# Seven-product down projection: another order of the products, and one activation sum on GpSimd

## The reference, cut to what matters

```python
x = x + _L0_ffn_ref(_layernorm(x, axis=-1), L0_ffn_w_gate, L0_ffn_w_up, L0_ffn_w_down)

def _L0_ffn_ref(x, w_gate, w_up, w_down):
    gate = jnp.einsum('bsd,hd->bsh', x, w_gate)
    up = jnp.einsum('bsd,hd->bsh', x, w_up)
    gated = jax.nn.silu(gate) * up
    return jnp.einsum('bsh,dh->bsd', gated, w_down)
```

## Time and profile before

| | us |
|---|---|
| runs, median of 3 | 1593.62 |
| runs, lowest to highest | 1592.47 to 1597.46 |
| profiled execution, its own time | 1592.21 |
| profiled execution, span | 1590.4 |
| TensorE busy in the span | 1528.7 (96%) |
| VectorE / ScalarE / GpSimd busy | 817.7 / 532.8 / 840.2 |

### The profile page before, as it was taken

The page is one execution under the profiler, slowest core; times in us unless marked ns, Lnnn a source line. Parts: engine busy times, 40 slices in busy tenths (PEclk is TensorE's granted clock), DMA queues, the critical chain, the costliest instruction groups (busy, mean ns, idle before and its releaser), DMA issues.

```text
span 1590.4 us, 23621 instructions
## 1 busy us (share of the span) xinstructions
PE 1528.7 (96%) x8204; PEld 1244.1 (78%) x8204; DVE 817.7 (51%) x1264; ACT 532.8 (34%) x1093; POOL 840.2 (53%) x643
## 2 busy tenths in 40 slices
PE   6999899999999999989999999999999999999998
PEld 5676688888888887777877877877877877877786
DVE  5666516235154187766256256256356346346346
ACT  3334423222132233333343343343343343343332
POOL 0000320211211302287797797797797797797794
PEclk9999999999999999999999999999999999999999
DMA  9663320110100100011111111121121221121212
GB/s 370 246 244 141 110 77 1 53 53 26 53 26 26 54 1 21 7 47 47 59 54 45 59 58 46 55 61 45 53 67 38 56 69 33 59 66 33 59 53 106
DMA packets 41798, 110.42 MB, mean 69 GB/s; under 512 B 4672, under 2 KB 4800, under 8 KB 39328
## 3 DMA queue, kind: packets, MB, share of 16 engines
q1 hardware_dynamic: 41328, 109.07, 20.3%
q10 hardware_dynamic: 432, 0.82, 0.2%
HBM read 105.68 MB, written 4.19 MB: 69 GB/s over the span
## 4 chain that ended last, share of the span: by engine, by line
PE 76%; DVE 13%; issue 5%; ACT 3%; POOL 1%; DMA 1%; DVEq 0%; SPq 0%; POOLq 0%; ACTq 0%
PE ps L1189 30%; PE ps L1209 12%; PE ps L821 8%; PE ps L823 7%; PE ps L822 7%; PE ps L852 3%; DVE h_sum L1578 2%; DVE ps L1570 2%; DVE x L1596 2%; PE ps L899 2%; PE ps L875 2%; DVE hid L1575 1%; PE ps L1027 1%; PE ps L827 1%; ACT b_hi L744 1%
## 5 line engine op out<-in xcount | busy, mean ns | idle before, releaser
L478 POOL TENSOR_TENSOR b_lo<-blk,b_hi 128x512 fp32r<-128x512 f32 x180 | 246.1, 1378 | 79.9 <-ACT b_hi L727 79.9
L447 POOL TENSOR_TENSOR w_lo<-raw,w_hi 128x2048 fp32r<-128x2048 f32 x18 | 83.5, 4640 | 325.7 <-ACT w_hi L592 325.7
L1596 DVE TENSOR_TENSOR x<-ps,x 128x1024 f32<-128x1024 f32 x210 | 242.1, 1209 | 2.0
L478 POOL TENSOR_TENSOR b_lo<-s_sum,b_hi 128x512 fp32r<-128x512 f32 x135 | 176.9, 1310 | 81.5 <-ACT b_hi L727 81.5
L1189 PE MATMUL ps<-xT_hi,b_hi 128*128 128x512 f32 x480 | 188.2, 392 | 2.1 <-DVE x L1496 2.1
L1189 PE MATMUL ps<-xT_hi,b_lo 128*128 128x512 f32 x480 | 187.0, 389 | 0.0
L1189 PE MATMUL ps<-xT_lo,b_hi 128*128 128x512 f32 x480 | 186.9, 389 | 0.0
L1209 PE MATMUL ps<-b_hi,b_hi 128*128 128x512 f32 x420 | 168.8, 402 | 17.3 <-DVE x L1596 13.6
L1209 PE MATMUL ps<-b_lo,b_hi 128*128 128x512 f32 x420 | 163.9, 390 | 0.0
L1209 PE MATMUL ps<-b_hi,b_lo 128*128 128x512 f32 x420 | 163.8, 390 | 0.0
L1567 DVE TENSOR_TENSOR hid<-ps,kept 128x512 f32<-128x512 f32 x60 | 41.5, 691 | 233.5 <-PE ps L1189 174.6
(11 more groups left out here) (162 smaller groups left out, 3249.8 us busy)
## 6 DMA issues: line engine op xcount, KB each, us to landing
blk<-in_blocks SPq DMA_DIRECT2D x180, 256.0 KB, 2.7
ctx<-in_ctx SPq DMA_DIRECT2D x64, 512.0 KB, 9.4
raw<-in_w SPq DMA_DIRECT2D x19, 1024.0 KB, 4.8
x<-in_x SPq DMA_DIRECT2D x8, 512.0 KB, 4.2
out<-x SPq DMA_DIRECT2D x16, 256.0 KB, 3.0
xn<-in_ext ACTq DMA_DIRECT2D x3, 128.0 KB, 7.8
mask<-in_mask ACTq DMA_DIRECT2D x1, 288.0 KB, 7.3
extT<-in_ext_t ACTq DMA_DIRECT2D x1, 128.0 KB, 4.8
```

What stands on the lines that cost most here:

```text
L447: pool.tensor_tensor(w_lo[wslot][:, :], raw[slot][:, :], w_hi[wslot][:, :].bitcast(F32), ALU.subtract).then_inc(split_done[slot], 1)
L478: pool.tensor_tensor(b_lo[slot][:, :], src[:, :], b_hi[slot][:, :].bitcast(F32), ALU.subtract).then_inc(block_lo, 1)
L1596: dve.tensor_tensor(part, ps[:, bank:bank + 2, :], part, ALU.add).then_inc(down_added, 1)
```

## The change

The blocks of the activations are named the other way round: A11, A12, A21, A22 are now hid blocks (0,0), (1,0), (0,1), (1,1), so that A11 is the block gathered first and A21 the last (before: (1,1), (0,1), (1,0), (0,0)). The weight's rows of blocks in HBM and `ADD_TO` follow. The order of the products becomes

| place | before | after |
|---|---|---|
| 0 | A11 b11 | A11 b11 |
| 1 | S1 (b12 - b11) | A12 b21 |
| 2 | S2 T2 | S2 T2 |
| 3 | (A12 - S2) b22 | S1 T1 |
| 4 | (A11 - A21) T3 | (A11 - A21) T3 |
| 5 | A12 b21 | (A12 - S2) b22 |
| 6 | A22 T4 | A22 T4 |

A12 - S2 is made by GpSimd, next to A11 - A21, and its result goes into the place of S1. It waits until VectorE has split S1 (`hid_lo` 4). T2 and T4 get a buffer of their own, `t_sum`, so T1 can stay in `s_sum` until place 3. VectorE's order from the second up gather on is: low(0), gather, low(1), gather, S1, S2, add(0,0), low(2), add(0,1), low(3), and the other adds. The number of products, matmuls, splits, adds, sums and loads is the same. The diff, cut to its core:

```diff
+        t_sum = sb_at("t_sum", "w_lo2", 6 * KB, [P, BLK])
...
-        DOWN_STARTS = (True, True, False, False, False, True, False)
-        ADD_TO = ((1, 0), (0, 1), (1, 1), (1, 1), (0, 1), (1, 0), (0, 0))
+        DOWN_STARTS = (True, True, False, True, False, False, False)
+        ADD_TO = ((0, 0), (0, 0), (0, 1), (1, 1), (1, 1), (0, 1), (1, 0))
+        ADDED_TWICE = {1: 0, 4: 3, 5: 2}
...
-                for slot, n in ((2, 14), (4, 17), (3, 18), (5, 19)):
-                    sync.wait_ge(block_lo, (c - 2) * WB + (n + 1))
-                    blocks(c, slot, slot + 1)
+                sync.wait_ge(sum_done, (c - 2) * 12 + 9)
+                blocks(c, 2, 3)
+                sync.wait_ge(block_lo, (c - 2) * WB + 19)
+                blocks(c, 3, 4)
+                sync.wait_ge(block_lo, (c - 2) * WB + 20)
+                blocks(c, 4, 5)
+                sync.wait_ge(sum_done, (c - 2) * 12 + 12)
+                blocks(c, 5, 6)
                 second_blocks(c)
-            for place in (3, 4, 5, 6):
+            for place in (1, 4, 5, 6):
...
             def down_unit(c):
                 b11, b12, b22, b21 = [blk[raw_of(2, i)] for i in range(4)]
-                for i in range(3):
+                for i in range(4):
                     pool.wait_ge(blk_full[raw_of(2, i)], raw_count(c, 2, i))
                 split_before(c, 14)
+                block_split(c, 14, b11)
                 combine(s_sum, b12, b11, ALU.subtract)
-                block_split(c, 14, b11)
-                block_split(c, 15, s_sum)
-                split_before(c, 16)
-                combine(s_sum, b22, s_sum, ALU.subtract)
+                block_split(c, 15, b21)
+                pool.wait_ge(sum_done, (c - 1) * 12 + 9)
+                combine(t_sum, b22, s_sum, ALU.subtract)
                 combine(b12, b22, b12, ALU.subtract)
-                block_split(c, 16, s_sum)
-                block_split(c, 17, b22)
+                block_split(c, 16, t_sum)
                 split_before(c, 17)
-                pool.wait_ge(blk_full[raw_of(2, 3)], raw_count(c, 2, 3))
-                combine(s_sum, b21, s_sum, ALU.subtract)
-                pool.wait_ge(hid_summed, (c - 1) * 3 + 1)
-                pool.tensor_tensor(hidden(hid, (1, 0)), hidden(hid, (1, 1)), hidden(hid, (1, 0)),
-                                   ALU.subtract).then_inc(hid_diff, 1)
+                combine(t_sum, b21, t_sum, ALU.subtract)
+                block_split(c, 17, s_sum)
+                pool.wait_ge(hid_summed, (c - 1) * 2 + 1)
+                hidden_sum(A21, A11, A21)
                 block_split(c, 18, b12)
-                block_split(c, 19, b21)
-                hidden_split(c, 4, hidden(hid, (1, 0)))
-                hidden_split(c, 5, hidden(hid, (0, 1)))
-                block_split(c, 20, s_sum)
-                hidden_split(c, 6, hidden(hid, (0, 0)))
-
+                pool.wait_ge(hid_summed, (c - 1) * 2 + 2)
+                pool.wait_ge(hid_lo, (c - 1) * 4 + 4)
+                hidden_sum(h_sum[0][:, :], A12, h_sum[1][:, :])
+                hidden_split(c, 4, A21)
+                block_split(c, 19, b22)
+                hidden_split(c, 5, h_sum[0][:, :])
+                block_split(c, 20, t_sum)
+                hidden_split(c, 6, A22)
+
+            def hidden_sum(dst, one, other):
+                pool.tensor_tensor(dst, one, other, ALU.subtract).then_inc(hid_diff, 1)
+
+            A11, A12, A21, A22 = [hidden(hid, part) for part in ((0, 0), (1, 0), (0, 1), (1, 1))]
...
                     block_high(c, 14 + i)
-                hidden_high(c, 0)
-                after_product(c, 10)
+                    if i == 1:
+                        after_product(c, 10)
+                        hidden_high(c, 0)
+                after_product(c, 12)
                 hidden_high(c, 1)
-                after_product(c, 12)
-                hidden_high(c, 2)
                 after_product(c, 13)
                 block_high(c, 17)
+                hidden_high(c, 2)
                 after_down(c, 0)
+                hidden_high(c, 3)
                 block_high(c, 18)
-                hidden_high(c, 3)
                 after_down(c, 1)
+                hidden_high(c, 4)
                 block_high(c, 19)
-                hidden_high(c, 4)
                 after_down(c, 2)
...
-            A11, A12, A21, A22 = [hidden(hid, part) for part in ((1, 1), (0, 1), (1, 0), (0, 0))]
+            A11, A12, A21, A22 = [hidden(hid, part) for part in ((0, 0), (1, 0), (0, 1), (1, 1))]
             with dve.Fori(1, NC) as c:
                 for i in range(4):
                     gather(c, 0, i)
...
                 gather(c, 1, 1)
                 low(c, 0)
                 gather(c, 1, 2)
-                dve.wait_ge(c_done, (c - 1) * 8 + 7)
-                combine_hidden(h_sum[0][:, :], A21, A22, ALU.add)
-                dve.wait_ge(hid_summed, (c - 1) * 3 + 1)
-                combine_hidden(h_sum[1][:, :], h_sum[0][:, :], A11, ALU.subtract)
                 low(c, 1)
                 gather(c, 1, 3)
+                dve.wait_ge(c_done, c * 8)
+                combine_hidden(h_sum[0][:, :], A21, A22, ALU.add)
+                dve.wait_ge(hid_summed, (c - 1) * 2 + 1)
+                combine_hidden(h_sum[1][:, :], h_sum[0][:, :], A11, ALU.subtract)
+                add(c, 0, 0)
                 low(c, 2)
-                dve.wait_ge(c_done, c * 8)
-                low_before(c, 2)
-                combine_hidden(h_sum[0][:, :], A12, h_sum[1][:, :], ALU.subtract)
-                add(c, 0, 0)
+                add(c, 0, 1)
                 low(c, 3)
-                add(c, 0, 1)
                 add(c, 1, 0)
                 add(c, 1, 1)
```

More of the change, by code:

```diff
@@ L718, in block_high @@
                 u, place = n // 7, n % 7
-                whole = {0: 0, 3: 2, 5: 3} if u == 2 else {0: 0, 3: 3, 5: 2}
+                whole = {0: 0, 1: 3, 5: 2} if u == 2 else {0: 0, 3: 3, 5: 2}
                 if place in whole:
@@ L723, in block_high @@
                 else:
-                    src = blk[raw_of(u, 1)] if place == 4 else s_sum
-                    done = {1: 1, 2: 2, 4: 3, 6: 4}[place]
+                    src = blk[raw_of(u, 1)] if place == 4 else t_sum if u == 2 and place != 3 else s_sum
+                    done = {3: 1, 2: 2, 4: 3, 6: 4}[place] if u == 2 else {1: 1, 2: 2, 4: 3, 6: 4}[place]
                     act.wait_ge(sum_done, (c - 1) * 12 + (4 * u + done))
@@ L735, in hidden_high @@
             def hidden_high(c, k):
[L736 to L741, removed]
+                src = (hidden(hid, (0, 0)), hidden(hid, (1, 0)), h_sum[1][:, :], h_sum[0][:, :],
+                       hidden(hid, (0, 1)), h_sum[0][:, :], hidden(hid, (1, 1)))[k]
+                if k in (2, 3):
+                    act.wait_ge(hid_summed, (c - 1) * 2 + {2: 2, 3: 1}[k])
+                elif k in (4, 5):
+                    act.wait_ge(hid_diff, (c - 1) * 2 + (k - 3))
                 else:
-                    act.wait_ge(c_done, (c - 1) * 8 + {0: 6, 5: 8, 6: 5}[k])
+                    act.wait_ge(c_done, (c - 1) * 8 + {0: 5, 1: 7, 6: 6}[k])
                 act.activation(b_hi[h_slot(k)][:, :], src, ACT.Copy).then_inc(hid_hi, 1)
@@ L1580, in low @@
             def low(c, k):
-                src = (hidden(hid, (1, 1)), h_sum[0][:, :], h_sum[1][:, :], h_sum[0][:, :])[k]
+                src = (A11, A12, h_sum[1][:, :], h_sum[0][:, :])[k]
                 dve.wait_ge(hid_hi, (c - 1) * HB + (k + 1))
@@ L1584, in low @@
                                   ALU.subtract).then_inc(hid_lo, 1)
-            def low_before(c, k):
-                dve.wait_ge(hid_lo, (c - 1) * 4 + k)
             def add(c, place, q):
@@ L1591, in add @@
                 dve.wait_ge(down_added, added(c - 1, 6, 1))
-                if place in (3, 4, 5):
-                    dve.wait_ge(down_added, added(c, {3: 2, 4: 1, 5: 0}[place], q))
+                if place in ADDED_TWICE:
+                    dve.wait_ge(down_added, added(c, ADDED_TWICE[place], q))
                 bank = DOWN_BANKS[place] + 2 * q
@@ L1684, in d_blocks @@
         part = np.asarray(w)[:, 2 * c * P:(2 * c + 2) * P].reshape(2, HALF, 2, P).transpose(2, 0, 3, 1)
-        return [part[1 - i, j] for i, j in ((0, 0), (0, 1), (1, 1), (1, 0))]
+        return [part[i, j] for i, j in ((0, 0), (0, 1), (1, 1), (1, 0))]
     blocks = []
```

## The result

| | before | after |
|---|---|---|
| median of five runs each, us | 1593.62 (1592.47 to 1597.46) | 1586.6 (1584.72 to 1587.83) |
| profiled execution, own time / span, us | 1592.21 / 1590.4 | 1584.72 / 1582.9 |
| TensorE / VectorE / GpSimd busy, us | 1528.7 / 817.7 / 840.2 | 1525.8 / 794.6 / 851.7 |

The ratio of after to before is 0.995, with a 95% interval of 0.9936 to 0.9965: 7 us faster, more than the 0.3% that can be told, but not the 27 us of the forecast.

What follows compares the result with a forecast made beforehand. TensorE, busy 96% of the span, was taken as the bound. Its down-step loss falls from 2.01 to 0.21 us, 1.80 a chunk times 15, 27 us: from 1593.62 to 1566.6 us, range 1562.5 to 1582.

Steps and rivals of the forecast that it cites:

- The loss and its place: Down step, products 1 and 2 behind VectorE's queue: 2.01 us lost a chunk, falling to 0.21.
- Who takes the turn: Down step, second sum against GpSimd's fourth: VectorE goes first and takes 0.69 us, GpSimd about 1.8.
- (a): Rival, down step: GpSimd takes the turn before VectorE's second sum; gain only 0.6 us a chunk, 1584.6 us; chance 0.12.
- (b): Rival, down step: a turn is lost earlier, around low(0); 1577 us if lost by half, 1583.7 if whole; chance 0.10.
- the alternation: Down step, earlier trace: of VectorE and GpSimd, the second waits, then takes 0.55 us (VectorE) or 1.15 (GpSimd).
- So the moved sum costs nothing, covered by that slack: GpSimd's queue, splits for products 4 to 6: least slack 1.3 us, so the added sum costs nothing.
- its signs of being wrong: A granted clock below 1.00, or a pause in the gate and up units, would make the forecast wrong elsewhere.
- Rival (c): GpSimd bounds the down step, its operations taking 1.79 us rather than 1.29: slower, 1606 us; chance 0.04.
- The rule against the move: The sum moved to GpSimd: the skill says shared read ports may give no gain; the prediction expected neighbouring adds to decide.
- The loads, the earlier stores and b21's earlier conversion: Still 12 block loads a chunk, four last-chunk stores earlier, b21 wanted earlier: all forecast to cost nothing.

Runs made afterwards that it cites:

- e6_no_third: The changed kernel with the third activation sum (A12 - S2) left out on GpSimd and S1 used in its place: 1570.21 us.
- e2_keeps: The changed kernel with ScalarE's copies keep(c,0,1) and keep(c,0,2) put ahead of the weight conversions that wait for GpSimd: 1563.39 us.
- e8_third_on_vector: e2_keeps with the third activation sum (A12 - S2) back on VectorE, between low(3) and add(1,0): 1589.49 us.
- e1_keep1: The changed kernel with only the copy keep(c,0,1) moved ahead of block_high(c,8) on ScalarE; keep(c,0,2) stays behind block_high(c,9): 1588.26 us.
- e7_split17_later: e2_keeps with GpSimd's split of block 17 moved behind the fourth activation sum: 1558.93 us.

## Why the prediction was wrong, point by point

- **The loss and its place, right.** 2.0 us a chunk in the down step, at products 1 and 2, behind VectorE's queue. The starts after show 1.69 of it gone; 1.80 was forecast. The remainder stands at product 3 (0.11 + 0.10, forecast 0.10 + 0.11), and 0.08 at product 2, to which I gave 0.2 to spare.
- **Who takes the turn, right.** From the timelines of VectorE and GpSimd after:

```profile
852.80 0.94 DVE L1591 TENSOR_TENSOR h_sum<-hid 128x512 f32<-128x512 f32 x1
853.77 0.69 DVE L1591 TENSOR_TENSOR h_sum<-h_sum,hid 128x512 f32<-128x512 f32 x1
...
853.82 1.80 POOL L547 TENSOR_TENSOR hid<-hid 128x512 f32<-128x512 f32 x1 [0.62 <-DVE h_sum L1591]
...
857.25 0.85 DVE L1596 TENSOR_TENSOR b_lo<-h_sum,b_hi 128x512 fp32r<-128x512 f32 x1
858.02 1.21 DVE L1606 TENSOR_TENSOR x<-ps,x 128x1024 f32<-128x1024 f32 x1
858.18 1.30 POOL L547 TENSOR_TENSOR h_sum<-hid,h_sum 128x512 f32<-128x512 f32 x1 [0.62 <-DVE b_lo L1596]
```

  VectorE was 0.05 us ahead and kept its 0.69; GpSimd took 1.80. The moved sum, beside an add that reads PSUM, took 1.30. Rivals (a) and (b) did not happen. That their times (1584.6, and 1583.7 at the end of (b)) lie near the 1586.6 measured is chance: both put the loss into the down step. The durations 0.94, 0.85 and 1.80 come from the alternation that the prediction read at 855.52 to 858.95 in the earlier trace rows.
- **The step that failed: "So the moved sum costs nothing, covered by that slack".** I followed GpSimd's queue through the down step and the next chunk's first two operations, and compared each with the product that uses it. Three things were wrong. I took comfort in GpSimd being "ahead in absolute time", by 0.45 us at its last split (866.8 against 867.25), while the same working has TensorE ahead by 1.80: against TensorE that is 1.35 us late, and 1.34 was measured. The cover has to be followed until the queue comes to rest, and in this kernel, behind the moved sum at 858.18, GpSimd's timeline has no idle time above 0.15 us until 893.69, 23 us into the gate and up units. And a late GpSimd operation reaches TensorE through whoever waits for it in order: here ScalarE's conversion of a block that TensorE needs only at product 8, with a copy behind it that product 4 needs. The rows that say so were in the trace of before (the copy ending at 883.71, 0.3 us ahead of its product, and the wait at 706.00), and I had not listed ScalarE's queue past the down step.
- **What that step cost.** The term "nothing" measured 1.32 us x 14 = 18.5 us; with it the sum gives a gain of 8.5 us and 1585.1, against 1586.6 measured. Of the 1.32 us, 1.16 goes when the moved sum is left out (39.51 against 38.35 in e6_no_third); the other 0.16 is left with TensorE reaching the gate unit sooner and no sum moved. The prediction did name a pause in the gate and up units among its signs of being wrong, and it read those units as free of pauses where the trace had 0.1 us (38.19 against 38.08).
- **Rival (c), right engine, wrong place.** GpSimd's lateness did become the bound, yet not by dearer operations and not at its own splits: it took 1.30 us beside the adds, as the earlier trace rows had it. e2_keeps shows that GpSimd was not short of time: its late sum only held up an urgent copy in ScalarE's queue.
- **The rule against the move.** The Trainium skill, "Perfetto Trace Analysis", section "Optimizing Scalar/DVE Operations", warns that work moved between these two engines may gain nothing. Here the move itself is worth 26 us (e8_third_on_vector against e2_keeps, the same in ScalarE's order). On GpSimd the sum met only adds, which read PSUM and one SBUF tensor, and took 1.30 us; on VectorE it took 1.67 us ahead of an add that TensorE waits for.
- The loads, the earlier stores and b21's earlier conversion cost nothing, as forecast: with ScalarE's order mended the gate and up units are at TensorE's pace, and behind the last matmul the span has 5.9 us where it had 6.2 (1582.9 - 1576.99, 1590.4 - 1584.18).

## What to carry to other kernels

Where an operation is moved to an engine with room to spare, follow that engine's queue until it next stands idle for longer than the operation takes, and at each step list who waits for it and what is queued behind that waiter; a copy that TensorE needs soon should not stand behind a conversion that waits for a slow engine and is needed late. A slack that shows no wait can still be only 0.3 us: compare the end of the last input with the start of its product, not idle times, and look whether one pass of the loop, here the first, already shows the wait. If a freed pause comes back a stage later, try all the paths from the late engine together, since mending one showed only the next (e1_keep1 against e2_keeps).

## What the runs showed of the hardware that was not expected

Which engine got the turn differed between two places that look alike on VectorE. In e8_third_on_vector a GpSimd split had started while low(3) still ran (859.26), and the sum, 0.04 us behind low(3), lost the turn and took 1.67 us, not 0.69: 0.98 us more. In the changed kernel the second sum, 0.03 us behind the first, kept its turn and its 0.69; GpSimd's sum there is released by that same first sum and started 0.05 later (853.82). What differs is that in the first place GpSimd's operation was already waiting; no run varies that alone.

The wait was free where GpSimd bore it: e7_split17_later has GpSimd's split of block 17 out of the way of VectorE's first sum, whose 0.94 us became 0.69, and TensorE has no pause. That one late split was worth 4.5 us of 1563.
